# Layer 0 of a graph-network kernel reads six row tiles only as transposed strips kept in SBUF

## What is computed

```
A = adj + eye(N);  D = 1 / sqrt(sum(A, axis=1))
A = A * D[:, None] * D[None, :]
x = layernorm(x + relu(A @ (x @ W) + b))
```

## Time and profile before

| | |
|---|---|
| median of 3 runs | 1450.9 us (1450.29 to 1452.09) |
| span of the profiled execution | 1449.1 us |
| that execution's own device time | not recorded apart; the runs' median lies 1.8 us above its span |
| PE, DVE, ACT, POOL busy | 92%, 63%, 38%, 13% of the span |
| HBM read | 316.94 MB, 221 GB/s over the span |
| first W0 product of layer 0 | 230.06 us after the start |

### The profile page before, as it was taken

How to read it: one execution, slowest core, us unless ns; L and a number is a source line. 1 busy time by engine, 2 the same in 40 slices (tenths; PEclk the granted TensorE clock), 3 DMA queues, 4 the chain that set the end, 5 groups by cost and what they waited for, 6 DMA issues and landing times.

```text
span 1449.1 us, 11441 instructions
## 1 busy us (share of the span) xinstructions
PE 1339.7 (92%) x4198; PEld 675.7 (47%) x4198; DVE 906.9 (63%) x1187; ACT 543.8 (38%) x469; POOL 187.7 (13%) x211
## 2 busy tenths in 40 slices
PE   3888886899989999999999999999999999999993
PEld 1333334444444444455655454644445444544451
DVE  4787777888865000003125363599878987898576
ACT  4444444867630000000111001455564565555333
POOL 0000002000020000000000000124431244113111
PEclk9999997899999999999899999999999999999997
DMA  9999993000026767758447339698876888688301
GB/s 380 427 426 416 419 390 107 2 0 0 0 96 175 196 192 196 193 150 275 149 164 236 105 109 325 211 363 327 307 281 252 329 304 310 229 306 329 141 0 50
DMA packets 78002, 321.27 MB, mean 222 GB/s; under 512 B 8685, under 2 KB 20588, under 8 KB 61036
## 3 DMA queue, kind: packets, MB, share of 16 engines
q1 hardware_dynamic: 77931, 320.40, 61.9%
HBM read 316.94 MB, written 3.43 MB: 221 GB/s over the span
## 4 chain that ended last, share of the span: by engine, by line
PE 82%; DMA 10%; DVE 5%; ACT 1%; issue 1%; SPq 0%; POOL 0%; ACTq 0%; DVEq 0%; POOLq 0%
PE ps L1321 29%; PE ps L1132 10%; PE ps L1169 10%; PE ps L1066 10%; DMA ring<-in_adjR 9%; PE ps L991 6%; PE ps L1126 5%; PE ps L1231 2%; PE ps L1342 1%; PE ps L1303 1%; PE ps L1150 1%; PE ps L1343 1%; DMA ring<-in_adjB 1%; PE ps L1106 1%; PE ps L1151 1%; PE ps L1190 1%
## 5 line engine op out<-in xcount | busy, mean ns | idle before, releaser
L1321 PE MATMUL ps<-arena,x 128*128 128x512 f32 (+1 forms) x1092 | 438.9, 562 | 2.9 <-ACT shared L894 1.6
L1321 PEld LDWEIGHTS ps<-arena,x 128*128 128x128 f32 x1092 | 206.1, 190 | 231.4 <-issue 225.2
L887 ACT ACTIVATE arena<-arena,bench 128x3328 f32<-128x3328 bf16 x78 | 239.8, 3075 | 188.8 <-PE ps L1321 176.4
L991 PE MATMUL ps<-ring,bench 128*128 128x512 f32 (+1 forms) x364 | 171.9, 617 | 51.1 <-DMA ring<-in_adjR 48.9
L1982 DVE TENSOR_TENSOR arena<-arena,ring 128x3328 f32<-128x3328 f32 x51 | 184.9, 3625 | 27.3 <-ACT arena L887 26.8
L1132 PE MATMUL ps<-ring,x 128*128 128x512 f32 (+1 forms) x364 | 176.2, 566 | 0.0
L1169 PE MATMUL ps<-ring,x 128*128 128x512 f32 (+1 forms) x364 | 152.1, 573 | 1.0 <-DMA ring<-in_adjB 1.0
L991 PEld LDWEIGHTS ps<-ring,bench 128*128 128x128 f32 x364 | 70.8, 206 | 130.6 <-issue 97.1
L1691 DVE SCALAR_TENSOR_TENSOR bench<-b,cols,ps 128x128 f32<-128x128 f32 x26 | 7.3, 343 | 183.1 <-PE ps L1106 183.1
L651 POOL TENSOR_TENSOR ring<-ring,nid 128x128 f32<-128x128 f32 x51 | 86.0, 1686 | 205.2 <-DMA ring<-in_adjR 205.2
L1126 PE MATMUL ps<-arena,shared 128*128 128x512 fp8e4 (+1 forms) x364 | 103.6, 366 | 6.1 <-DVE shared L1496 6.1
(11 more groups left out here) (289 smaller groups left out, 1427.8 us busy)
## 6 DMA issues: line engine op xcount, KB each, us to landing
ring<-in_adjR SPq DMA_DIRECT2D x77, 1664.0 KB, 8.7
ring<-in_adjB SPq DMA_DIRECT2D x312, 256.0 KB, 3.1
arena<-in_adjR SPq DMA_DIRECT2D x27, 1664.0 KB, 8.4
shared<-in_adj SPq DMA_DIRECT2D x7, 1664.0 KB, 13.4
es<-in_adj SPq DMA_DIRECT2D x7, 1664.0 KB, 13.4
xT<-in_adj SPq DMA_DIRECT2D x6, 1664.0 KB, 13.0
y<-in_adj SPq DMA_DIRECT2D x6, 1664.0 KB, 13.4
ring<-in_adjB SPq DMA_DIRECT2D x52, 128.0 KB, 2.3
```

The costliest lines, as they stand in the source:

```text
L887: A_(E[n % 3], below[n % 3], ACT.Exp, bias=tt_[:, t * HEADS + k:t * HEADS + k + 1], scale=-WIN).then_inc(e_exp, 1)
L991: op = mm(ps[:, b, 0:w], lhsT=scaled[:, t % 4], rhs=turned_tile[t % 2][:, o_:o_ + w], start=(t == 0), stop=(t == TILES - 1))
L1321: last = mm(ps[:, b, 0:w], lhsT=x[:, t], rhs=E[n % 3][:, o_:o_ + w], start=(t == 0), stop=(t == TILES - 1))
```

## The change

The six last row tiles (20 to 25) are no longer loaded. Their rows are columns 2560 to 3327 of adj.T, so they are in every turned tile. Each turned tile is now loaded as 2560 columns (into `ring`) and a strip of 768 columns (`adjS`, into `arena`, two of them into `gru`), and the strips of all 26 tiles are loaded three a step in steps 0 to 8 and stay. `strip_columns` multiplies ones by each strip, into bank 7 and the upper half of bank 6, which gives the six tiles' row sums along the columns; `strip_rows` on DVE picks out the diagonal of that to have them on partitions, and ACT takes all six roots at once. DVE takes minima over strips in place of the six row tiles. Tiles go downwards, since tile t's entry of `pos8` overwrites tile t+1's strip, with a strip tile (25 to 20) among them at steps 10, 13, 16, 19, 22 and 24. In a step PE starts with blocks 5 and 6, which need only the strip, save in steps 9 and 25. The pattern is made in two pieces, of which the first waits for PE's end of the step before.

```diff
+STRIP = 6
+PLAIN = TILES - STRIP
+SC = STRIP * P
+MC = NP - SC
+STRIPS_A_STEP = 3
+FILLED = -(-TILES // STRIPS_A_STEP)
+FIRST_STRIP = FILLED + 1
+ORDER = [19, 18, 17, 16, 15, 14, 13, 12, 11, 10, 25, 9, 8, 24, 7, 6, 23, 5, 4, 22, 3, 2, 21, 1, 20, 0]
...
-        WEIGHTS_A_TILE, WEIGHTS_PE, WEIGHTS_VE = 4, 8, 9
+        WEIGHTS_A_TILE, WEIGHTS_PE, WEIGHTS_VE = 4, 12, 13
...
+        PITCH = NP // 4
+        STRIP_ORDER = list(range(PLAIN - 1, -1, -1)) + list(range(TILES - 1, PLAIN - 1, -1))
+        STRIP_AT = {j: i for i, j in enumerate(STRIP_ORDER)}
+        gru_flat = gru[:].rearrange("p a f -> p (a f)")
+        gb_flat = gb[:].rearrange("p e a f -> p (e a f)")
+
+        def strip(j):
+            if j in (0, PLAIN):
+                return piece(gru_flat, SC if j == 0 else 0, SC)
+            return piece(arena, (j - 1) * PITCH, SC)
+
+        def strips_of(s):
+            return STRIP_ORDER[STRIPS_A_STEP * s:STRIPS_A_STEP * (s + 1)]
+
+        def strip_value(c):
+            return 16 * len(strips_of(c))
+
+        def strip_loaded(eng, j):
+            c = STRIP_AT[j] // STRIPS_A_STEP
+            eng.wait_ge(ring_in[c], strip_value(c))
+
+        def plain_until(s):
+            return sum(j < PLAIN for j in ORDER[:s])
+
+        def summed_until(s):
+            return plain_until(s + 1) + (s >= FIRST_STRIP)
...
-            def nat_load(t):
-                if t >= 4:
-                    sp.wait_ge(nat_used, t - 3)
-                sp.dma_start(nat[t % 4], d["adj"][t // 2, :, t % 2]).then_inc(nat_in[t % 4], 16)
+            def nat_load(n):
+                if n >= 4:
+                    sp.wait_ge(nat_used, n - 3)
+                j = PLAIN - 1 - n
+                sp.dma_start(nat[n % 4], d["adj"][j // 2, :, j % 2]).then_inc(nat_in[n % 4], 16)
...
-            for t in range(TILES):
-
-                for dst, src in early[WEIGHTS_A_TILE * t:WEIGHTS_A_TILE * (t + 1)]:
+            for s, j in enumerate(ORDER):
+
+                for dst, src in early[WEIGHTS_A_TILE * s:WEIGHTS_A_TILE * (s + 1)]:
                     sp.dma_start(dst, src).then_inc(weights_in, 16)
-                if t >= 2:
-                    sp.wait_ge(tile_used, t - 1)
-                    sp.wait_ge(pos_done, t - 1)
-                sp.dma_start(turned_tile[t % 2], d["adjR"][t]).then_inc(tile_in[t % 2], 16)
-                if t + 2 < TILES:
-                    nat_load(t + 2)
+                for q in strips_of(s):
+                    sp.dma_start(strip(q), d["adjS"][q]).then_inc(ring_in[s], 16)
+                if s >= 2:
+                    sp.wait_ge(tile_used, s - 1)
+                    sp.wait_ge(pos_done, s - 1)
+                sp.dma_start(turned_tile[s % 2][:, 0:MC], d["adjR"][j, :, 0:MC]).then_inc(tile_in[s % 2], 16)
+                if j < PLAIN and plain_until(s) + 2 < PLAIN:
+                    nat_load(plain_until(s) + 2)
...
+            for n in range(PLAIN):
+                j = PLAIN - 1 - n
+                act.wait_ge(nat_in[n % 4], (n // 4 + 1) * 16)
+                if n == 0:
                     act.wait_ge(consts, 1)
-                A_(nat[t % 4], nat[t % 4], ACT.Copy, accum_out=rs[:, t:t + 1]).then_inc(summed, 1)
-                act.wait_ge(summed, t + 1)
-                A_(sd[:, t:t + 1], rs[:, t:t + 1], ACT.Sqrt, bias=ones[:, 0:1]).then_inc(sd_done, 1)
+                A_(nat[n % 4], nat[n % 4], ACT.Copy, accum_out=rs[:, j:j + 1]).then_inc(summed, 1)
+                act.wait_ge(summed, n + 1)
+                A_(sd[:, j:j + 1], rs[:, j:j + 1], ACT.Sqrt, bias=ones[:, 0:1]).then_inc(sd_done, 1)
+                if n + 1 == FIRST_STRIP:
+
+                    act.wait_ge(strip_sums, 1)
+                    A_(sd[:, PLAIN:], rs[:, PLAIN:], ACT.Sqrt, bias=ones[:, 0:1]).then_inc(sd_done, 1)
...
+            def strip_columns(s):
+                for q in strips_of(s):
+                    i = STRIP_AT[q]
+                    strip_loaded(pe, q)
+                    mm(ps[:, 7, :], lhsT=ones[:], rhs=strip(q)[:, 0:MAX_WIDTH], start=(i == 0), stop=(i == TILES - 1))
+
+                    last = mm(ps[:, 6, GW:2 * GW], lhsT=ones[:], rhs=strip(q)[:, MAX_WIDTH:SC], start=False, stop=(i == TILES - 1),
+                              skip_group_check=True)
+                    if i == TILES - 1:
+                        last.then_inc(strip_summed, 1)
+
+            for s, t in enumerate(ORDER):
+                first, final = s == 0, s == TILES - 1
+                if s == WEIGHTS_PE:
+                    pe.wait_ge(strip_sums, 1)
                     weight_products()
-                if t == WEIGHTS_VE + 3:
+                if s == WEIGHTS_VE + 3:
                     spread_w2()
-                pe.wait_ge(xs_done, t + 1)
-                pe.wait_ge(tile_in[t % 2], (t // 2 + 1) * 16)
-                for b, (o_, w) in enumerate(BLOCKS):
+                pe.wait_ge(xs_done, s + 1)
+                strip_loaded(pe, t)
+                for k, b in enumerate((0, 1, 2, 3, 4, 5, 6) if final or s == FILLED else (5, 6, 0, 1, 2, 3, 4)):
+                    o_, w = BLOCKS[b]
                     at = t % BT * P
 
                     def itself():
-                        mm(ps[:, b, at:at + P], lhsT=scaled[:, t % 4], rhs=ident[:], start=False, stop=False)
-                    if t and t // BT == b:
+                        mm(ps[:, b, at:at + P], lhsT=scaled[:, s % 4], rhs=ident[:], start=False, stop=False)
+                    if b == 0:
+                        strip_columns(s)
+                        pe.wait_ge(tile_in[s % 2], (s // 2 + 1) * 16)
+                    if b == 6 and s == FILLED:
+                        pe.wait_ge(strip_sums, 1)
+                    if not first and t // BT == b:
                         itself()
-                    op = mm(ps[:, b, 0:w], lhsT=scaled[:, t % 4], rhs=turned_tile[t % 2][:, o_:o_ + w], start=(t == 0),
-                            stop=(t == TILES - 1))
-                    if t == TILES - 1:
+                    moving = strip(t)[:, o_ - MC:o_ - MC + w] if o_ >= MC else turned_tile[s % 2][:, o_:o_ + w]
+                    op = mm(ps[:, b, 0:w], lhsT=scaled[:, s % 4], rhs=moving, start=first, stop=final)
+                    if final:
                         op.then_inc(last_block, 1)
-                    elif b == NB - 1:
+                    elif k == NB - 1:
+                        if first:
+                            itself()
                         op.then_inc(tile_used, 1)
...
+            def scan(s):
+                t = ORDER[s]
+                ve.wait_ge(sd_done, summed_until(s))
                 v.reciprocal(D[:, t:t + 1], sd[:, t:t + 1]).then_inc(D_done, 1)
-                ve.wait_ge(D_done, t + 1)
-                if t >= 4:
-                    ve.wait_ge(tile_used, t - 3)
-                v.tensor_scalar(scaled[:, t % 4], x[:, t], D[:, t:t + 1], None, ALU.mult).then_inc(xs_done, 1)
-                ve.wait_ge(summed, t + 1)
-                ge(ve, diag_done, t)
-                v.tensor_reduce(mn[:, t:t + 1], nat[t % 4], AX.X, ALU.min)
-                v.tensor_tensor(hb[:, 0], nat[t % 4][:, t * P:(t + 1) * P], ident[:], ALU.mult).then_inc(nat_used, 1)
-                ve.wait_ge(nat_used, t + 1)
+                ve.wait_ge(D_done, s + 1)
+                if s >= 4:
+                    ve.wait_ge(tile_used, s - 3)
+                v.tensor_scalar(scaled[:, s % 4], x[:, t], D[:, t:t + 1], None, ALU.mult).then_inc(xs_done, 1)
+                ge(ve, diag_done, s)
+                if t < PLAIN:
+                    n = plain_until(s)
+                    ve.wait_ge(summed, n + 1)
+                    v.tensor_reduce(minima[:, n:n + 1], nat[n % 4], AX.X, ALU.min)
+                    v.tensor_tensor(hb[:, 0], nat[n % 4][:, t * P:(t + 1) * P], ident[:], ALU.mult).then_inc(nat_used, 1)
+                    ve.wait_ge(nat_used, n + 1)
+                else:
+                    strip_loaded(ve, t)
+                    at = (t - PLAIN) * P
+                    v.tensor_tensor(hb[:, 0], strip(t)[:, at:at + P], ident[:], ALU.mult).then_inc(diag_prod, 1)
+                    ve.wait_ge(diag_prod, 1 + s - plain_until(s) + 1)
                 v.tensor_reduce(dg[:, t:t + 1], hb[:, 0], AX.X, ALU.add).then_inc(diag_done, 1)
 
-            def pattern(t):
-                ve.wait_ge(tile_in[t % 2], (t // 2 + 1) * 16)
-                v.tensor_scalar(pos8[:, t], turned_tile[t % 2], 0.0, None, ALU.is_gt, saturate=False).then_inc(pos_done, 1)
+            def strip_minima(s):
+                for q in strips_of(s):
+                    strip_loaded(ve, q)
+                    at = PLAIN + STRIP_AT[q]
+                    v.tensor_reduce(minima[:, at:at + 1], strip(q), AX.X, ALU.min)
...
+            def strip_rows():
+                ve.wait_ge(strip_summed, 1)
+                ve.wait_ge(tile_used, FILLED)
+                of = gb_flat[:, 0:SC].rearrange("p (t f) -> p t f", t=STRIP)
+                for lo, hi, bank, at in ((0, BT, 7, 0), (BT, STRIP, 6, GW)):
```

(72 more changed lines are left out.)

4 lines of the change are left out of this document (removed).

## The result

The changed kernel takes **1444.28 us** (median of 4 runs, 1439.39 to 1445.22) against 1450.81 for the kernel before in the same comparison (4 runs, 1450.29 to 1452.09): a ratio of 0.9945, 95% interval 0.9927 to 0.9962. By that ratio it is 8.0 us faster, by the medians 6.5; forecast were 12, with a time of 1439 and a range of 1430 to 1448. The time lies within the range, 5 us above the forecast. Both kernels' single runs lie several us apart, so the stage is read from the profiles.

A forecast was written before the change was run, and what follows sets the result against it. Transfers were taken to bound stage 0, ending at 230.06 us; 118.5 (through step 9) + 93.1 (PE) + 1.2 (small products) + 4.2 (waits) + 0.8 (clock) = 217.8, 12.3 us less, giving 1439 us, range 1430 to 1448.

The forecast's parts named there:

- Bound before, and its shift: Stage 0, before W0's products: transfers bind at 4.06 us a load, so fewer bytes shorten it until another engine takes over.
- Strips: Loads of 768 columns in steps 0 to 8: 1.05 us each, between 0.94 and 1.23.
- Products with ones, DVE, ACT: Fill, steps 0 to 8: PE 9.69 us a step, DVE 9.6, ACT six sums fewer; transfers bind at 10.33.
- Fill and step 9: Steps 0 to 9: step 8 ends at 110.0 us, step 9's tile lands at 112.7, step 9 ends at 118.5.
- Waits after the fill: Steps 10 to 25: PE waits 1.0 us for each of four later strip tiles, 0.2 for the last: 4.2.
- PE now binds: Steps 10 to 25: PE needs 5.82 us a step, 93.1 in all, and sets the pace.
- a share near 0.85: Sign after 118 us: the DMA engines' share near 0.85, with PE above 90% busy.
- Transfers stay the bound: Rival for the whole stage: transfers bind throughout, 21.5 us saved, kernel at 1429 us; chance 0.10.
- The clock at each of six gaps: Rival: clock halves at steps 9, 13, 16, 19, 22 and 25, costing 9.4 us more; kernel 1446 us; chance 0.12.
- The two-deep ring's round trip: Rival, steps 9 to 25: issue waits for step s-2, 8.11 us a plain step; kernel 1462 us; chance 0.05.
- A fixed cost of 2 to 3 us per load in the fill: Rival: each strip pays 3.0 us, fill grows by 78 us, kernel 1517 us; the skill's figure is 2.0; chance 0.02.
- It moves as one block: Everything after the stage keeps its length, so the kernel gains the stage's 12.3 us.

The follow-up runs named there:

- e8: The kernel before the change, with three places each for turned tiles and row tiles and no strips; ratio 0.9996 to the kernel before.
- e9: The changed kernel with the products of ones and strip done twice for 24 of the 26 strips; 1470.8 us, ratio 1.0141 to the kernel before.
- e1: The changed kernel with a third place for turned tiles, taken from the row tiles' four; 1436.17 us, ratio 0.989 to the kernel before.
- e0_again: The changed kernel run once more with nothing altered; 1442.45 us, ratio 0.9941 to the kernel before.
- e3: The changed kernel with each strip loaded as two transfers of 384 columns; 1442.17 us, ratio 0.994 to the kernel before.
- e2: The changed kernel without the products with ones for 24 of the 26 strips; 1444.12 us, ratio 0.9952 to the kernel before.
- e4: The changed kernel with three places for turned tiles and 24 of 26 strips not multiplied by ones; 1432.76 us, ratio 0.9888 to the kernel before.

## Why the prediction was right or wrong

**Bound before, and its shift: right.** Transfers bound the stage, and six row tiles less made it shorter. e8 shows the same from the other side: a third place does not help that kernel.

**Strips: right, a little high.** A fill step of 10.08 us less 4.06 and 3.12 leaves 0.97 us a strip (taken: 1.05, bounds 0.94 to 1.23). The prediction's straight line gives 3.18 for the 2560 columns, not the 3.12 it writes, which is the stage's own rate; with 3.18 a strip is 0.95. The Trainium skill, "DMA: Bandwidth & Descriptors", section "Anatomy of one DMA — SWDGE (gpsimd) path", has some 2.0 us fixed beside bytes/436 GB/s, an estimated 2.9 us for a strip. In SP's queue, which isn't empty during the fill, the trace does not agree with such a cost for each load: 0.97 us. With halved strips (192 KB) the fill moves at 409 GB/s against 418.

**Products with ones, DVE, ACT: right.** The products are 104 with 42.7 us of busy time by their own durations, which overlap; e9's step of 13.55 us confirms 3.87 a step. The minimum over 768 columns takes 942 ns (0.95), the pattern 0.55 + 1.49. DVE is busy 34.9 of 40 us in the fill. That it isn't the bound is read from the DMA share of 1.02 and from e1, where the wait for its pattern is a step looser and step 9's tile lands at the same time; no experiment took work from it.

**Fill and step 9: right, in part by luck.** Step 9's tile landed 1.5 us early (111.19 against 112.7), since eight fill steps took 10.08 and not 10.33 us each. The half clock at step 9, put in at even odds with 0.8, came and took some 1.6; in e0_again, the same program, it did not come there. Step 9 ends near 118.8, against 118.5 + 0.8 = 119.3: two errors that nearly cancel.

**Waits after the fill: here the sum fell short, and "PE now binds" did not hold.** From 118.8 the stage takes 102.9 us, not 93.1 + 1.2 + 4.2 = 98.5: 4.4 more; less the 0.5 by which step 9 ended early, they are the 3.9 that the stage missed (221.7 against 217.8). The term is the prediction's "I take 1.0 for each of the four later strip tiles and 0.2 for the last tile: 4.2". For the strip tiles it was sound: tile 24 (step 13) landed 14.7 us after the issue of step 12's tile (124.70 to 139.44), against 14.6, and the four waited 0.75, 0.47, 0.71 and 0.71 us, 2.6 together (4.0 in e0_again). What it put at nothing is the plain tile ahead of each strip tile, at steps 12, 15, 18 and 21: 0.23, 1.31, 1.02 and 0.96, 3.5 together (2.7 in e0_again). With 0.29 for the last tile that makes the 6.4. Tile 6 shows how:

```profile
144.08 0.33 SPq L508 DMA_DIRECT2D ring<-in_adjR  x1
```

It was issued at 144.08, when step 13 had ended, behind tile 7 (step 14) and a row tile, and PE took it up at 152.45: some 8.3 us from issue to landing, while PE has 7.1 in hand (a step of 5.82 and the strip blocks' 1.3). The queue was short of work just before: tile 7 could be issued only when step 12 had ended, and in the two microseconds from 138 on it moved 182 and 266 GB/s.

The rest of the 8.8 us between e1 and the changed kernel stands in the timeline too. A wait is counted from the end of the group before, which lies 0.16 us after the point where the next group starts if nothing holds it (1.45 us at 143.88, the next at 145.17), and the first products after a gap take 0.10 longer (4.56 for ten, against 4.45 at 120.21). That is 0.26 a gap: 2.3 for nine, and with the 6.4 of waits 8.7. In e1, with no gap, the stage runs from step 9's end at 118.7 to 212.8, 94.1 us, where the prediction has 93.1 + 1.2 = 94.3: PE's part of the sum was right.

The sum per step hid this: "plain steps load 7.2, strip steps 3.12 only; PE needs 5.82" reads as if PE had the greater work. Over the group of three that repeats it is 7.2 + 7.2 + 3.1 = 17.5 us of transfers against 3 x 5.82 = 17.5 of PE, and the group took 19.7. The prediction's own sign, "a share near 0.85", is a mean over all that follows the fill; in the groups its figures give 17.5/18.4 = 0.95, and the windows have 0.96 and 0.95. Two chains of equal length with two places between them lose here at each hand-over; with three, e1 shows both full and no wait.

**The rivals.** "Transfers stay the bound" was half true: they are level with PE. "The clock at each of six gaps" did not come: it fell at step 9 alone, and in e0_again not there but once at 198 us, after a wait of 2.08 us. The two-deep ring's round trip was the right mechanism with a wrong price: I gave it 8.11 us a step where it costs 19.7/3 = 6.6, against 5.8 without it, and so called it a slowdown with 0.05 where it was a part of the gain lost. Its sign, a mean of 7.06 us a step from step 9 on, is measured at (221.75 - 108.8)/17 = 6.64. A fixed cost of 2 to 3 us per load in the fill: refuted by e3.

**"It moves as one block": right but for the clock.** The rest is 1218.0 to 1219.5 us in eight profiles, the kernel before among them, and 1220.0 to 1223.4 in four, the changed kernel's first among them. In the four, two stretches at the lower clock near 690 and 740 us last 13.7 and 10.2 us instead of 10.2 and 6.8. The windows of the changed kernel and of e0_again, which are the same program:

```profile
660.00:760.00 100.00, 98.08 (x471) 56.81 (x470) 19.04 (x66) 12.63 (x23) 3.63 (x8) 0.88 0.57 183
```

```profile
660.00:760.00 100.00, 98.08 (x485) 56.11 (x484) 21.78 (x70) 12.63 (x23) 4.74 (x11) 0.91 0.61 196
```

The clock is not all of it: e1's window has the mean clock of the changed kernel's, 0.88, and its rest is 2.6 us longer, which I did not settle. Of the 5.6 us between forecast span (1436.8) and measured span (1442.4), 1.6 lie in the rest, and 4.0 in the stage. That the runs of one kernel lie 2 to 7 us apart may have the same source; their clocks over time are not recorded, and it stays open.

## What to carry to other kernels

Where an edit brings two resources level, compare their work over the group of steps that repeats, not step by step, and count the places between them: transfers and PE with the same work over three steps needed a third place here. The same place was worth nothing while transfers clearly bound (e8: 0.9996) and 0.5% once the two were level (e1: 0.989 against 0.9941). Look at the steps beside the one where you expect the wait, too: half of the waits fell on them. Added work goes free where another resource binds, but only up to the difference: the same products cost the stage 3 us at most once, and 25 more when doubled. The best version here is the change with three places, 1.1% under the kernel before.

## What the runs showed of the hardware

- Loads of 384 KB, and even of 192 KB, among larger ones in a queue that isn't empty hardly lower its rate: 418 and 409 GB/s with 28% of the bytes in such loads, against 427 with 1664 KB loads alone.
- A wait of 2.2 to 2.4 us at the same place, step 9, was followed by the lower clock in the changed kernel, e1 and e3 (four products in 3.58, 3.25 and 3.65 us), and not in e0_again, e2 and e4 (1.96, 1.95 and 1.96 us). The changed kernel and e0_again are one program with the same wait of 2.38 us, and PE was busy for 37.36 us of 80 to 120 in both; what decided it stays open. A mean clock of 0.87 in e2's fill cost no time, since PE had room.
- The rest of the program, the same work in each profile, varies by up to 5.4 us, in part with the length of the stretches at the lower clock.
